# A decoder's convolution taps made between the experts' tiles, and the combination of experts joined with the norm behind it

## The reference, cut to what matters

```
x = layernorm(x + L0_attention(x))
x = layernorm(x + L0_cross(ctx, x))
x = layernorm(x + L0_ffn(x, Wr, W1, W2))      # 8 experts, the best 2 of them for each token
x = layernorm(x + L1_attention(x))            # top 64 keys, heads mixed before and after
x = layernorm(x + L1_modulated(x, ctx))       # holds the convolution (s4d) below
x = layernorm(x + L1_ffn(x))
# s4d: for feature d and lag l
K[d, l] = 2 Re sum_n dC[d, n] * exp(dtA[d, n] * l)      # the taps: 256 features x 512 lags
y = irfft(rfft(x) * rfft(K))
```

## Time and profile before

| | |
|---|---|
| median of 3 runs | 3711.43 us (3710.67 to 3717.41) |
| the profiled execution's own time | 3717.24 us |
| its span, first to last instruction | 3715.2 us |
| granted TensorE clock, mean | 0.813 |
| the sort's scatters | 656.5 to 698.1 us |
| experts' stage | 704.7 to about 1022 us |
| combining stage | 1024.7 to 1114.8 us |
| norm | 1115.6 to about 1136.7 us |
| first load of the attention | 1136.91 us |

### The profile page before, as it was taken

The page is one execution under the profiler, slowest core; times in us unless marked ns, Lnnn a source line. Parts: engine busy times, 40 slices in busy tenths (PEclk is TensorE's granted clock), DMA queues, the critical chain, the costliest instruction groups (busy, mean ns, idle before and its releaser), DMA issues. The chain is left out here.

```text
span 3715.2 us, 40807 instructions
## 1 busy us (share of the span) xinstructions
PE 2823.8 (76%) x11784; PEld 1837.2 (49%) x11784; DVE 2403.8 (65%) x7562; ACT 1112.4 (30%) x2880; POOL 990.2 (27%) x1221
## 2 busy tenths in 40 slices
PE   4754896399956767776777678756467889999999
PEld 2322564277743445544554456434433446666666
DVE  4995564455321799989989998999757425212112
ACT  1112562133302333443343334332232023221221
POOL 2550000300030345454544454445422210000000
PEclk7555997699956678787868786866777999999999
DMA  2000002355522221221122112211020041212212
GB/s 90 0 0 15 6 1 82 130 161 169 155 81 74 83 80 41 84 63 67 53 73 72 59 54 70 64 55 33 5 77 1 0 97 59 67 52 74 67 52 68
DMA packets 180762, 235.36 MB, mean 63 GB/s; under 512 B 35761, under 2 KB 138869, under 8 KB 180286
## 3 DMA queue, kind: packets, MB, share of 16 engines
q1 hardware_dynamic: 177470, 224.37, 19.1%
q0 software_dynamic: 3072, 8.39, 0.7%
HBM read 170.57 MB, written 62.13 MB: 63 GB/s over the span
## 5 line engine op out<-in xcount | busy, mean ns | idle before, releaser
L2063 DVE MATCH_REPLACE8 a_rest<-a_best,a_rest 128x416 f32<-128x416 f32 (+54 forms) x1308 | 602.9, 468 | 0.0
L2071 DVE MAX8 a_best<-a_rest 128x8 f32<-128x416 f32 (+54 forms) x1308 | 564.3, 472 | 0.0
L1746 PE MATMUL a_pat<-a_kp,a_probs 128*128 128x128 f32 x1344 | 290.6, 390 | 203.7 <-POOL a_kp L1965 198.4
L1746 PEld LDWEIGHTS a_pat<-a_kp,a_probs 128*128 128x128 f32 x1344 | 258.1, 287 | 285.9 <-POOL a_kp L1965 262.8
L2004 POOL TENSOR_SCALAR a_probs<-a_mixed,a_best 128x120 f32<-128x120 f32 (+12 forms) x208 | 285.6, 1373 | 331.2 <-DVE a_best L2075 303.4
L1727 PE MATMUL a_psc<-a_kT,branch 64*128 64x264 f32 (+3 forms) x640 | 227.7, 613 | 161.7 <-ACT a_stage L1829 160.9
L3174 DVE TENSOR_TENSOR tl_hT<-tl_act_out,tl_gate 128x512 f32<-128x512 f32 x128 | 88.6, 692 | 385.9 <-ACT tl_act_out L3042 385.8
L1737 PE MATMUL a_pmix<-a_rows,a_kpre 128*128 128x264 f32 (+41 forms) x528 | 187.2, 485 | 84.9 <-ACT a_mixed L1862 80.1
L1727 PEld LDWEIGHTS a_psc<-a_kT,branch 64*128 64x128 f32 x640 | 119.4, 262 | 252.0 <-ACT a_stage L1829 226.8
L2956 PE MATMUL tl_py<-tl_w,tl_hT 128*128 128x256 f32 x1024 | 241.6, 379 | 0.0
L2937 PE MATMUL tl_ph<-xT,tl_w 128*128 128x512 f32 x512 | 240.7, 592 | 0.0
(11 more groups left out here) (418 smaller groups left out, 5267.2 us busy)
## 6 DMA issues: line engine op xcount, KB each, us to landing
f_w<-in_L_ffn_W SPq DMA_DIRECT2D x39, 1024.0 KB, 5.8
tl_gate<-l_gates SPq DMA_DIRECT2D x256, 128.0 KB, 2.9
l_scores<-a_stage SPq DMA_DIRECT2D x32, 528.0 KB, 2.7
l_scores<-a_stage SPq DMA_DIRECT2D x32, 400.0 KB, 2.4
l_scores<-a_stage SPq DMA_DIRECT2D x32, 272.0 KB, 2.1
f0o_w<-in_L_ffn_W SPq DMA_DIRECT2D x8, 1024.0 KB, 12.5
sorted_x<-z_blank SPq DMA_DIRECT2D x1, 4992.0 KB, 15.6
f_xs<-sorted_x SPq DMA_DIRECT2D x39, 128.0 KB, 5.4
```

Source lines behind the costliest of these rows:

```text
L1746: ins = pe.matmul(pat[:, at + c, :], probs[:, g % 4, c * P:(c + 1) * P], kp[:, g % 4, :], start=True, stop=True)
L2063: last[a] = signal(dve.match_replace(rest[:, a, 0:wd], best[:, a, q - 1, :], rows_of[a] if q == 1 else rest[:, a, 0:wd], GONE))
L2071: last[a] = signal(dve.max(best[:, a, q, :], rest[:, a, 0:wd]))
```

## The change

The matmuls that make the taps go into the experts' stage: after the second product of tile j, where j is 5, 9, ... 33, TensorE makes the 32 taps of chunk j//4 - 1, waiting for its factors; VectorE copies them a tile later into `K.taps`, which now lives over all four stages. The combination and the norm behind it become one stage, `l0_combine_and_norm`, ordered by batch: the gated outputs are added directly to x, then statistics, root, scaling and turning of that batch follow. TensorE's and ScalarE's orders put batch 0 between the fourth and fifth transform, and batches 1 to 3 behind the eighth. `norm_stage` is no longer called after `l0_ffn`. The arithmetic's amount stays, but for the separate product and the separate addition of branch to x.

```diff
+    STEPS = 7                                  # ConvolutionKernel
...
+        K.taps = sb("taps", [P, NT, D])        # l0_ffn
         l0_experts(nc, G, R, K)
-        l0_combine(nc, G, R, K)
+        l0_combine_and_norm(nc, G, R, K)
...
+        pk = ps("pk", [LO, CW, HI])            # l0_experts
+        made = K.steps[0]
...
+                def taps(c):
+                    pe.wait_ge(K.dve_steps, made + K.STEPS * (c + 1))
+                    if c >= 1:
+                        pe.wait_ge(taps_read, c)
+                    for i in range(CW):
+                        ins = pe.matmul(pk[:, i, :], K.V[:, CW * c + i, :], K.U[:, CW * c + i, :], start=True, stop=True)
+                    ins.then_inc(tapped, 1)
...
                     out(j)
+                    if j % K.PIECES == 1 and 1 <= j // K.PIECES <= CHUNKS:
+                        taps(j // K.PIECES - 1)
...
+                    c = j // K.PIECES - 1
+                    if j % K.PIECES == 2 and 0 <= c < CHUNKS:
+                        dve.wait_ge(tapped, c + 1)
+                        for a in range(4):
+                            ins = dve.tensor_copy(K.taps[32 * a:32 * a + 32, :, CW * c:CW * c + CW],
+                                                  pk[:, :, :].rearrange("l c (j a) -> l a j c", a=4)[:, a])
+                        ins.then_inc(taps_read, 1)
                     if j // K.PIECES < CHUNKS:
                         K.piece(dve, j // K.PIECES, j % K.PIECES)
...
+                def turn(b):                   # l0_combine_and_norm, TensorE
+                    pe.wait_ge(x_ready, NT * (b + 1))
+                    for k in range(KD):
+                        n = b * KD + k
+                        if n >= 2:
+                            pe.wait_ge(copied, n - 1)
+                        for q in range(NT):
+                            ins = pe.transpose(pT[n % 2][:, q, :], G.x[:, b * NT + q, k * P:(k + 1) * P], G.ident[:])
+                        ins.then_inc(turned, 1)
+
+                pe.wait_ge(dft_in, 16)
+                for m in range(FT):
+                    transform(m)
+                turn(0)
+                for m in range(FT, 2 * FT):
+                    transform(m)
+                for b in range(1, B):
+                    turn(b)
...
+                for m in range(FT):            # ScalarE
+                    keep(m)
+                root(0)
+                copies(0)
+                for m in range(FT, 2 * FT):
+                    keep(m)
+                for b in range(1, B):
+                    root(b)
+                    copies(b)
...
+                for b in range(B):             # VectorE
+                    dve.wait_ge(G.fetched[b], 16 * TOP0 * NT)
+                    for n in range(TOP0):
+                        for t in r:
+                            ins = dve.scalar_tensor_tensor(G.x[:, t, :], y[:, n, t, :], R.gates[:, n, t:t + 1],
+                                                           G.x[:, t, :], ALU.mult, ALU.add)
+                        step(ins)
+                    for t in r:
+                        ins = dve.bn_stats(stats[:, t, :], G.x[:, t, :])
+                    step(ins)
+                    for t in r:
+                        ins = dve.bn_aggr(mv[:, t, :], stats[:, t, :])
+                    step(ins)
+                    dve.tensor_scalar(rstd[:, rr], mv[:, rr, 1], EPS, None, ALU.add).then_inc(moments, 1)
+                    dve.wait_ge(rooted, b + 1)
+                    step(dve.reciprocal(rstd[:, rr], std[:, rr]))
+                    for t in r:
+                        dve.tensor_scalar(G.x[:, t, :], G.x[:, t, :], mv[:, t, 0:1], rstd[:, t:t + 1],
+                                          ALU.subtract, ALU.mult).then_inc(x_ready, 1)
...
             recycle(nc)
-            norm_stage(nc, G, f"n{i + 1}", add=stage is not l1_attention)
+            if stage is not l0_ffn:
+                norm_stage(nc, G, f"n{i + 1}", add=stage is not l1_attention)
```

More of the change, by code:

```diff
@@ L2617, with l0_combine_and_norm @@
 ES, FS = 2, 512
-def l0_combine(nc, G, R, K):
+def l0_combine_and_norm(nc, G, R, K):
     with ExitStack() as ctx:
-        sb, ps, sem = buffers(nc, ctx, "sp")
-        kl = sb("kl", [P, NT, D])
-        pk = [ps(f"pk{i}", [LO, 32, HI]) for i in range(2)]
+        sb, ps, sem = buffers(nc, ctx, "cn")
+        stats = sb("stats", [P, TT, 6])
+        mv = sb("mv", [P, TT, 2])
+        std = sb("std", [P, TT])
+        rstd = sb("rstd", [P, TT])
         pf = [ps(f"pf{i}", [P, 512]) for i in range(2)]
-        summed, copied, stored, weighed = sem("summed"), sem("copied"), sem("stored"), sem("weighed")
-        dft_in, spectrum, kept = sem("dft_in"), sem("spectrum"), sem("kept")
-        N = D // 32
+        pT = [ps(f"pT{i}", [P, NT, P]) for i in range(2)]
+        dft_in, spectrum, kept, stored = sem("dft_in"), sem("spectrum"), sem("kept"), sem("stored")
+        moments, rooted, x_ready = sem("moments"), sem("rooted"), sem("x_ready")
+        turned, copied, dve_steps = sem("turned"), sem("copied"), sem("dve_steps")
         room = R.w1[:].rearrange("p e k f -> p (e k f)")
@@ L2645, in _, with transform @@
             def _(pe):
[L2646 to L2655, removed]
+                def transform(m):
                     if m >= 2:
@@ L2658, in _ @@
                     for k in range(NT):
-                        ins = pe.matmul(pf[m % 2][:, 0:D], dft[:, k, m * P:(m + 1) * P], kl[:, k, :],
+                        ins = pe.matmul(pf[m % 2][:, 0:D], dft[:, k, m * P:(m + 1) * P], K.taps[:, k, :],
                                         start=(k == 0), stop=(k == NT - 1))
                     ins.then_inc(spectrum, 1)
+                def turn(b):
[7 more added lines that the diff above has]
+                        ins.then_inc(turned, 1)
@@ L2663, in _, with keep, root @@
+                pe.wait_ge(dft_in, 16)
[6 more added lines that the diff above has]
+                    turn(b)
             @block.scalar
             def _(act):
-                for m in range(2 * FT):
+                def keep(m):
                     act.wait_ge(spectrum, m + 1)
                     act.copy(kf[:, m, :], pf[m % 2][:, 0:D]).then_inc(kept, 1)
+                def root(b):
+                    r = slice(b * NT, (b + 1) * NT)
+                    act.wait_ge(moments, b + 1)
+                    act.activation(std[:, r], rstd[:, r], ACT.Sqrt).then_inc(rooted, 1)
@@ new lines, in copies @@
+                def copies(b):
+                    for k in range(KD):
+                        n = b * KD + k
+                        act.wait_ge(turned, n + 1)
+                        act.copy(G.xT[:, k, b * S:(b + 1) * S], pT[n % 2][:].rearrange("p a b -> p (a b)")
+                                 ).then_inc(copied, 1)
+                for m in range(FT):
[4 more added lines that the diff above has]
+                    keep(m)
@@ L2669, in _ @@
+                for b in range(1, B):
+                    root(b)
+                    copies(b)
             @block.vector
             def _(dve):
[L2671 to L2685, removed]
+                step = chain(dve, dve_steps)
@@ new lines, in _ @@
+                for b in range(B):
+                    r = range(b * NT, (b + 1) * NT)
+                    rr = slice(b * NT, (b + 1) * NT)
+                    dve.wait_ge(G.fetched[b], 16 * TOP0 * NT)
[16 more added lines that the diff above has]
+                                          ALU.subtract, ALU.mult).then_inc(x_ready, 1)
```

1 line of the change is left out of this document (added).

## The result

On the same chip the kernel after took 3693.97 us (median of 9 runs, 3685.53 to 3700.82) and the kernel before 3713.75 (9 runs, 3703.7 to 3720.45). The ratio is 0.9945, with an interval of 0.9935 to 0.9955: faster by 19.8 us, where 39.8 were forecast. The direction was right and the time lies in the range, near its upper end. It is near the time of rival A (3692), not that of the main case (3671.6).

What follows compares the result with a forecast made beforehand. TensorE bounds the experts' stage; taps, transforms and spectrum store stand in series in the combining stage. Replacing 112.2 us by 54.7 and adding 17.7 for taps gives -39.8, from 3711.4 to 3671.6 us; range 3664 to 3697.

Steps and rivals of the forecast that it cites:

- rival A: New combining stage: transforms crawl beside the gathers, delaying batch 1's root; stage 75.4 us, time 3692; chance 0.30.
- the main case: Whole kernel: the walk as it stands, 39.8 us saved, time 3671.6, own range 3664 to 3680; chance 0.51.
- Taps in the experts' stage: Experts' stage: 512 tap records on TensorE, paid in full, add 17.7 us, bounds 16.1 and 29.2.
- rival B: Experts' stage: small matmuls and waits let TensorE's clock fall; taps cost 29.2 us, time 3683 to 3690; chance 0.07.
- D: Experts' stage: taps trickle there too, making the kernel slower; at 10 us a chunk time 3734; chance 0.03.
- The chain by batch: Combining stage and norm: batches follow one another at 7.1 us of VectorE each; attention starts after 54.7 us, not 112.2.
- Rival C: Combining stage: VectorE holds up GpSimd, so the last gather comes 5 to 7 us late; time 3676; chance 0.07.
- Rival E: Attention's start: the change buys nothing because its first loads or another queue decide anyway; chance 0.02.
- the 41.5 us of trickling: Old combining stage: TensorE's slow stretch beside the gathers, left out of the cost of the moved taps.
- undisturbed 10.0 us per four: New combining stage: each four transforms take 10.0 us, as before, ending at 1044.0 and 1059.0.
- a gap without releaser in the transforms: New combining stage: a wait in the transforms with nothing shown to end it would prove the prediction wrong.
- part 2: Experts' stage: tap copies on VectorE, 1.1 us in one of four tiles, are hidden; 9.0 us in all otherwise.

Runs made afterwards that it cites:

- the sixth: The kernel before, unchanged, run again on chip 5 for its trace; 3672.76 us, once.
- the fourteenth: The kernel after with the roots of batches 1 to 3 moved ahead in ScalarE's order, on chip 3; 3681.2 us, ratio 0.9919 to the kernel before.
- the seventh: The kernel after with the roots of batches 1 to 3 moved ahead in ScalarE's order, on chip 5; 3676.56 us, ratio 1.0006 to the kernel before.
- the tenth: The kernel after, but taps made at the combining stage's head and copied by ScalarE, on chip 3; 3696.83 us, ratio 0.9952 to the kernel before.
- the fifteenth: The kernel before with GpSimd's gathers held until all taps are copied, on chip 3; 3702.64 us, once.

## Why the prediction came out as it did

**Taps in the experts' stage: right.** +17.3 against +17.7 (18.1 by the stage's own length), at 0.99 of the clock. Neither rival B nor D came. The starts are 32 ns apart. The forecast's 31.4 divides by 31 records where there are 30 distances; by 30 it is 32.3, 0.5 us more in the sum. The floor of about 25 ns of the Trainium skill (TensorE: Matmul & The Clock Gate, Wait — 56ns, not 53.3ns?) was not reached in this stage.

**The chain by batch: right as arithmetic.** Without the lag the stage takes 53.6 us (54.7 forecast); a batch takes 7.2 us (7.1). Rival C did not come: in the trace of the kernel after, the last gather was issued 40.0 us after the stage's start (1082.05), 0.5 us later than in the earlier trace rows, and the pitch stayed at 1.25 to 1.44 us. Rival E did not come.

**The step that failed** is the one in brackets under the taps' cost: "the 41.5 us of trickling do not belong to their work". True, but the walk then let them vanish: it gave the new stage, which has the same gathers at its head, transforms at their undisturbed 10.0 us per four. I held against rival A that transforms ask for few records. The records were indeed no trouble. What is held back beside the gathers is the signal at the end of the work, and the transforms have one every 1.7 us, each of which someone waits for. Rows on record already had it: in the earlier trace rows VectorE sees the end of the first 64 records only at 1031.07, named "remote", 6.4 us into the stage; in the sixth it is 2.9 (1027.61). The prediction names this row and draws nothing from it. Its own sign of being wrong, a gap without releaser in the transforms, came, one engine further on: in ScalarE's copies.

The 17.1 us that were missed (71.8 against 54.7) fall in two parts. 10.2 us are the root of batch 1 behind the late copies: with the roots earlier the stage takes 61.6 us (1040.12 to 1101.69), and 10.5 us are measured in the time. The remaining 7 are late signals on the path itself, as the same order takes 54.3 us without the lag (the seventh): in the fourteenth root 0 comes 26.4 us after the stage's start, in the seventh 20.1, and copies with late signals still stand ahead of root 1. Rival A had the place and the consequence right (root of batch 1, 75.4 us, 3692) but its mechanism, records that start late, is not what happened to the transforms: the first 32 start 0.3 us apart. That its time is met within 2 us is in part luck. Its stage is 3.6 us too long, and by the traces the change should have won 23.1 us (112.2 - 71.8 - 17.3), where the medians differ by 19.8. (Its "about 36 of 64" is 38 by its own rate, and the tile's 8.0 us under part 2 are 8.1; nothing hangs on either.)

**What the forecast could not see** is that the number it subtracted from held in one condition only. The 112.2 us are 71.8 on another chip, in the same kernel. There the sum has to be 17 + 53.6 - 71.8, about nothing, and nothing was measured. "Faster" is right with the lag alone.

**Still open.** Why gathers by index hold back the engines' signals, and why on one chip and not on two others. A strong rival to a fault of the chip is the recording itself: where signals are late, records of updates are missing too. It was not tried: every run here, the timed ones too, has a recorded span. So it is not known whether the lag, and with it the gain of the change, is there without recording. The Trainium skill (NOTIFIC — the notification-queue block, Constraints, capacities, measured rates) says that emitting a record costs the engine nothing, and that the block can hold some 500 records while its way out is slower than the engines. A start at full pace and then a crawl, as in the tenth, would fit a store that fills up, and so would single records 0.7 us or a multiple of it apart; no run here shows what it holds. Gathers spread over the experts' stage, or issued in another size, were not tried.

## What to carry to other kernels

A gap that names no releaser is not free time to be won by moving what stands in it: ask what runs beside it, and charge the same gap to whatever takes its place. Put small steps that another engine waits for (here the roots) ahead of those whose signal may be late; it cost nothing without the lag and gave 10 us with it. And before an effect of 0.5% is explained from one trace, run the kernel before on another chip: here its time moved by 38 us, twice the effect. Look as well at what the trace lacks: transfers without a time to landing were the mark of this condition in the very first trace.

## What the runs showed of the hardware

- On one chip gathers by index (32, one each 1.25 us) held back the engines' signals by up to 24 us (the fifteenth); TensorE's dense row of small matmuls fell to one record in 0.7 to 2.8 us (the tenth). It ended 5 to 6 us after the last gather was issued (4.9 in the kernel after, 6.3 in the fifteenth). On two other chips nothing of it is seen, and the kernel before takes 36 to 38 us less. All of it was seen with recording on.
- In the same condition the traces keep 74 to 171 of the gathers' 512 semaphore updates (494 to 512 elsewhere), and all of those of plain loads through the same queue.
- Plain loads of the same 128 rows cost GpSimd 0.53 us each to issue (17.03 us for 32), SyncE 0.49 (15.57 for 32), against 1.25 for the gathering ones.
- The records of a small float32 matmul (32 by 16) start 52 ns apart in a stage where the clock is mostly at its lower level (0.52 over the 26.8 us of taps in the sixth) and 32 ns apart at 0.99 (the kernel after).
